# The first layer of the pair network in four column tiles of 32 in place of two of 64

## What is computed

```python
h = jnp.einsum('bsd,fd->bsf', xn, W1)                                # 128 features
pair = jax.nn.relu(h[:, :, None, :] - h[:, None, :, :] + b1)
pair = jax.nn.relu(jnp.einsum('bijf,gf->bijg', pair, W2) + b2)       # 128 -> 64: the first layer
sim = jnp.einsum('bijg,og->bijo', pair, W3)[..., 0] + b3[0]          # 64 -> 1: the second layer
_, top_idx = jax.lax.top_k(sim, k_sparse)                            # k_sparse = 51
```

## Time and profile before

| | us |
|---|---|
| median of three runs | 3159.86 |
| lowest, highest | 3156.14, 3160.17 |
| span of the profiled execution, first to last instruction | 3157.4 |
| TensorE busy, share of the span | 3004.7, 95% |
| VectorE busy | 2335.5, 74% |
| ScalarE busy | 1771.7, 56% |
| GpSimd busy | 1059.2, 34% |
| mean granted TensorE clock, share of full speed | 0.976 |

### The profile page before, as it was taken

How to read it: one execution, slowest core, us unless ns; L and a number is a source line. 1 busy time by engine, 2 the same in 40 slices (tenths; PEclk the granted TensorE clock), 3 DMA queues, 4 the chain that set the end, 5 groups by cost and what they waited for, 6 DMA issues and landing times. The chain is left out here.

```text
span 3157.4 us, 45069 instructions
## 1 busy us (share of the span) xinstructions
PE 3004.7 (95%) x16681; PEld 1670.8 (53%) x16681; DVE 2335.5 (74%) x4298; ACT 1771.7 (56%) x2897; POOL 1059.2 (34%) x881
## 2 busy tenths in 40 slices
PE   6999999999999899999899989989999987999999
PEld 3334334333433344444478868854444435887787
DVE  6988998999898877777366676655766776667665
ACT  4988888888888546666633333323443443334332
POOL 1000000000000264543155565613545554565653
PEclk9999999999999889999999999999999988999999
DMA  2000000000000000000111111124333311112111
GB/s 75 1 1 11 1 1 11 1 1 11 1 1 1 1 1 2 1 2 1 31 44 54 50 41 57 47 92 109 88 91 77 101 34 53 44 54 74 54 53 44
DMA packets 105759, 112.18 MB, mean 36 GB/s; under 512 B 8963, under 2 KB 74500, under 8 KB 105157
## 3 DMA queue, kind: packets, MB, share of 16 engines
q1 hardware_dynamic: 102918, 108.61, 12.2%
q10 hardware_dynamic: 2624, 0.69, 0.1%
HBM read 84.76 MB, written 20.97 MB: 33 GB/s over the span
## 5 line engine op out<-in xcount | busy, mean ns | idle before, releaser
L730 DVE TENSOR_SCALAR pair_in<-key_words,row_words 128x512 f32<-128x512 f32 x1792 | 726.1, 480 | 44.7 <-PE ps L617 40.7
L815 ACT ACTIVATE pair_mid<-ps,row_bias 128x512 f32<-128x512 f32 x896 | 588.2, 688 | 133.5 <-PE ps L617 116.1
L617 PE MATMUL ps<-pair_in,w_hi 128*64 128x512 f16 x3584 | 584.7, 390 | 8.6 <-DVE pair_in L730 8.3
L1081 DVE TENSOR_REDUCE maxes<-ps 128x2 f32<-128x1024 f32 x256 | 303.2, 1221 | 94.5 <-PE ps L994 93.4
L843 POOL TENSOR_SCALAR_AFFINE_SELECT sim<-sim 128x512 f32<-128x512 f32 x16 | 9.9, 620 | 1051.9 <-ACT sim L832 1051.9
L617 PEld LDWEIGHTS ps<-pair_in,w_hi 128*64 128x64 f16 x3584 | 202.3, 108 | 301.8 <-issue 66.4
L617 PE MATMUL ps<-pair_in,w_lo 128*64 128x512 f16 x1792 | 352.3, 388 | 0.0
L1491 PE MATMUL ps<-ffn_b_hi,ffn_a_hi 128*128 128x512 f32 x904 | 287.6, 400 | 24.8 <-DVE ffn_up L1579 9.9
L1125 ACT ACTIVATE ex<-ps 128x512 f32<-128x512 f32 x448 | 243.2, 595 | 118.2 <-PE ps L1013 117.4
L1491 PE MATMUL ps<-ffn_b_lo,ffn_a_hi 128*128 128x512 f32 x904 | 283.5, 395 | 2.4 <-DVE ffn_b_lo L1561 2.4
L1491 PE MATMUL ps<-ffn_b_hi,ffn_a_lo 128*128 128x512 f32 x904 | 282.8, 394 | 0.7 <-POOL ffn_a_lo L1722 0.7
(11 more groups left out here) (240 smaller groups left out, 5344.6 us busy)
## 6 DMA issues: line engine op xcount, KB each, us to landing
ffn_raw_up<-in_w_ffn SPq DMA_DIRECT2D x64, 512.0 KB, 4.0
ffn_raw_down<-in_w_ffn SPq DMA_DIRECT2D x64, 256.0 KB, 2.7
q_stack<-halves SPq DMA_DIRECT2D x48, 256.0 KB, 5.1
k_stack<-halves SPq DMA_DIRECT2D x48, 256.0 KB, 5.9
halves<-hi_b SPq DMA_DIRECT2D x16, 512.0 KB, 2.7
halves<-lo_b SPq DMA_DIRECT2D x16, 512.0 KB, 3.6
out<-x SPq DMA_DIRECT2D x4, 1024.0 KB, 4.5
x<-in_x SPq DMA_DIRECT2D x6, 512.0 KB, 6.9
```

The source lines that it names most:

```text
L617: s = nc.tensor.matmul(ps[F2 * half:F2 * half + F2, bank + which, :], w_part[:, :], words.rearrange("p (s two) -> p s two", two=2)[:, :, o ...
L730: s = nc.vector.tensor_scalar(p.pair_in[:, (4 * n + i) % N_PAIR, :], p.key_words[:, b % 2, :], p.row_words[:, b % 2, row:row + 1], None, A ...
L815: nc.scalar.activation(p.pair_mid[:, n % NG, which, :], ps[:, bank + which, :], ACT.Relu, bias=bias).then_inc(p.mid_made, 1)
L1081: nc.vector.tensor_reduce(maxes[:, c % 2, 2 * pair:2 * pair + 2, h], ps[:, 2 * pair:2 * pair + 2, :], AX.X, ALU.max).then_inc(maxes_made, 1)
```

## The change

In the first layer each matmul of 64 outputs becomes two of 32 outputs, with the lower and the upper 32 columns of the same weights and the same input. A pass is then four matmuls and four weight loads where it was two and two. The three f16 passes and the f32 product are all changed so. Waits, semaphores, PSUM contents, the other engines' programs and the order of steps stay as they are.

```diff
                     if r % 2 and g and which:
                         pe.wait_ge(p.act_row_made, 8 * tile + r // 2 + 1)
-                        for half in range(2):
-                            s = nc.tensor.matmul(ps[F2 * half:F2 * half + F2, bank + which, :], p.w2_scaled[:, :],
+                        for quarter in range(4):
+                            half, at_w = quarter // 2, 32 * (quarter % 2)
+                            s = nc.tensor.matmul(ps[32 * quarter:32 * quarter + 32, bank + which, :],
+                                                 p.w2_scaled[:, at_w:at_w + 32],
                                                  p.pair_in[:, (4 * n + 2 + half) % N_PAIR, :], start=True, stop=True)
                         s.then_inc(p.pair_out, 1)
                         continue
                     for part, (w_part, of_word) in enumerate(((p.w2_hi, 1), (p.w2_lo, 1), (p.w2_hi, 0))):
-                        for half in range(2):
+                        for quarter in range(4):
+                            half, at_w = quarter // 2, 32 * (quarter % 2)
                             words = p.pair_in[:, (4 * n + 2 * which + half) % N_PAIR, :].bitcast(F16)
-                            s = nc.tensor.matmul(ps[F2 * half:F2 * half + F2, bank + which, :], w_part[:, :],
+                            s = nc.tensor.matmul(ps[32 * quarter:32 * quarter + 32, bank + which, :],
+                                                 w_part[:, at_w:at_w + 32],
                                                  words.rearrange("p (s two) -> p s two", two=2)[:, :, of_word],
                                                  start=part == 0, stop=part == 2)
```

## The result

| | before | after | ratio |
|---|---|---|---|
| median, us | 3160.02 (four runs, 3156.14 to 3161.14) | 3141.78 (four runs, 3138.70 to 3143.91) | 0.9943, 95% interval 0.9929 to 0.9956 |
| span of the profiled execution | 3157.4 | 3137.5 | |

The change is 18.2 us faster, 0.57%; 3139 was forecast, 20.7 less. The profiled execution of after is the one of 3138.70, the low end of its four runs, so the two spans lie further apart (19.9) than the medians.

The account below looks back on a forecast made before the run. TensorE's own sequence was taken to bound the pair network's stage. 30.2 - 0.8 - 2.6 - 6.1 = 20.7 us less gave 3139 us, with an 8-in-10 range from 3129 to 3175.

Parts of the forecast that it names:

- Width changes removed: Between the pair network's two layers: 110 places lose 0.255 us each, 18 save 0.12 on the way in; 30.2 us gained.
- Row_bias given back: Row_bias, now the only 64-wide work, stands between 32-wide work in three batches; 3 x 0.255 = 0.8 us lost.
- Twice the matmuls: First layer: four matmuls a pass cost 0.9 ns more on each of 2688 passes, and the f32 ones; 2.6 us lost.
- Weight loads: First layer: twice as many loads, half as wide, fit within a pass of 0.225 us; no cost.
- VectorE's stretch: Two stretches where TensorE waits for VectorE: 20 blocks' saving, 5.1 us, not gained; 1.0 for first batch and scores; 6.1.
- ScalarE: Its free time in each block shrinks from 0.8 to 0.54 us; no cost to the kernel.
- The slower rival: Handing out first-layer matmuls becomes the bound: at 60 ns each, 43 us more and the kernel at 3173; chance 0.15.

Follow-up runs that it names:

- Experiment 1: Kernel before with only the f32 unit of each block in four tiles of 32, f16 passes still 64 wide: 3161.84 us, ratio 1.0006.
- experiment 3: Changed kernel with the f16 matmuls of a pass issued in order 0, 2, 1, 3: 3143.38 us; separately, with row_bias also in four tiles: 3139.66 us, ratio 0.9932.
- experiment 2: Every f16 matmul split into two of 256 columns: 3141.36 us in the changed kernel, 3162.7 us in the kernel before.

## Why the prediction was right

The terms are held against the stage, which lost 19.75 us where 20.7 was forecast.

1. **Width changes removed** (30.2 us): right in cause, place and size. Experiment 1 moves the gap with the width. From plain blocks and hand-overs the round trip is 0.26 to 0.27 us where 0.255 was taken, which makes 31 to 32 us.
2. **Row_bias given back** (0.8): 0.29 us in each of three blocks, 0.9.
3. **Twice the matmuls** (2.6): the pass went from 0.2254 to 0.2276, 2.2 ns where the f32 rows gave 0.9; 5.9 us if all 2688 passes paid what those of the last 27 blocks do. This term was undersized by up to 3.3 us and is the largest error; it is why a plain block takes 7.354 and not the 7.31 that was to be seen. Point 1, which came out 1 to 2 us larger, and point 5, 0.7 smaller, took most of it back, and that they did is luck. The value taken for the price was that of one stagger of the tiles, and with another it is nearly met (0.2259 in experiment 3).
4. **Weight loads** (nothing): right. Twice as many again cost nothing in the changed kernel and 1 ns a pass in the one before (experiment 2).
5. **VectorE's stretch** (6.1): right, and to be seen in rows of the changed kernel: two waits of VectorE with none between them, TensorE's last wait, and the busy times of the stretch (columns as in the earlier trace rows):

```profile
309.73 0.70 DVE L743 MAX8 best<-sim 128x8 f32<-128x517 f32 x1 [4.26 <-POOL sim L847]
424.59 0.89 DVE L734 TENSOR_SCALAR pair_in<-key_words,row_words 128x512 f32<-128x512 f32 x2 [1.51 <-PE ps L620]
```

```profile
390.02 0.41 PE L620 MATMUL ps<-pair_in,w_hi 128*32 128x512 f16 x4 [0.87 <-DVE pair_in L734]
```

```profile
309.70:390.00 80.30, 76.37 (x1100) 36.76 (x1092) 79.08 (x201) 70.00 (x110) 1.32 (x3) 1.00 0.01 2
```

From its first `max` to the end of TensorE's last wait for it are 80.29 us. Before, the same two places were 317.34 and 397.63, also 80.29. Ten blocks in which TensorE had less to do took exactly as long. The whole loss is 25.18 - 19.75 = 5.4 us, where 5.1 and part of 1.0 had been set aside. The first batch's stretch, for which part of the 1.0 us was meant, showed no wait; the waits of the other two stretches began sooner instead. TensorE's idle time in the stretch grew by less than I wrote, from 2.4 to 3.9 us (busy for 76.37 of 80.30) and not to 5. A part of that is that ten plain blocks save 2.2 us (0.218 each) and not 2.6; the rest stays open.
6. **ScalarE** (nothing): right. Its pause in a block fell to 0.53 us, 0.54 had been worked out:

```profile
933.86 4.82 ACT L819 ACTIVATE pair_mid<-ps,row_bias 128x512 f32<-128x512 f32 x7 [0.53 <-PE ps L620]
```

The slower rival, handing out matmuls as a bound, rested on a burst of four transposes at 60 ns each. Experiment 2 ran matmuls with their loads at 28 ns for a whole stage. So the pace of that burst is no limit of the hand-out. The Trainium skill, on its page TensorE: Matmul & The Clock Gate, under "Wait — 56ns, not 53.3ns?", gives about 62 ns a MATMUL with hardware decode off. The 28 ns here do not fit that case. The same section of the Trainium skill states that starts never follow each other by less than some 25 ns, with either decode path. This case does not agree for tiles side by side: the four second-layer matmuls of a pass start about 7 ns apart in the trace of before. The 28 ns are an average over a set of four that share 107 ns of columns (256 at 2.4 GHz), so the columns set them, and the floor does not show.

Together: 31 to 32 us for the widths, less 0.9, 5 to 6 and 5.4, leave 19 to 21; the stage shows 19.75.

## What to carry to other kernels

Where two kinds of narrow matmuls alternate, bring them to one tile width, even at the price of more instructions: a change of width cost 0.12 to 0.15 us each way here, and handing out a matmul with its load every 28 ns was not a bound. When the engine that sets the time gets faster, look in the trace for the stretches where another engine has no wait between two points: there the saving is nothing until work moves out, and it must move to where that engine waits, not merely be spread out.

## What was not expected of the hardware

- An f16 pass costs about 0.44 ns a column (0.2254 us for 512) whether it is one set of matmuls or two of half the length, while an f32 pass of 512 columns (0.429 us) takes less than twice as long.
- The starts of the four tiles either keep their distance or drift against each other, and the pass costs 0.2259 us or 0.2276 with the same instructions, according to work that ended 100 us and more before.
